# State-space scans of a fused two-layer kernel: three small jobs move between POOL, DVE, ScalarE and TensorE

## The chip, the cores and the metric

One core of a Trainium2 chip runs the whole kernel in one launch. The metric is the device time in microseconds, as the median of several executions. All engines named here are of that core: TensorE (PE, its weight loads PEld), VectorE (DVE), ScalarE (ACT), GpSimd (POOL) and SyncE (SP), which only issues DMAs.

## The reference, cut to what matters

The model has two layers: a tokeniser, attention and a mixture of experts in the first, and in the second a selective state-space block (called attn in the names) and a quantised feed-forward block. There are 16 sequences of 113 tokens with 256 channels, and 16 states per channel. The change touches only the state-space block:

```python
def _L1_attn_ref(x, ...):
    xr = x @ in_proj_w.T + in_proj_b
    x_in, res = jnp.split(xr, 2, axis=-1)
    xc = conv_general_dilated(x_in..., conv_w, ...)      # causal, 4 taps, one filter per channel
    xc = jax.nn.silu(xc + conv_b)
    ssm = xc @ x_proj_w.T + x_proj_b
    delta, Bp, Cp = jnp.split(ssm, [DTRANK, DTRANK + DSTATE], axis=-1)
    delta = jax.nn.softplus(delta @ dt_proj_w.T + dt_proj_b)
    A = -jnp.exp(A_log)
    dA = jnp.exp(delta[..., None] * A)
    dBu = delta[..., None] * Bp[:, :, None, :] * xc[..., None]
    _, ys = jax.lax.associative_scan(op, (dA, dBu), axis=1)   # h[t] = dA[t] * h[t-1] + dBu[t]
    y = (ys * Cp[:, :, None, :]).sum(-1) + xc * D_param
    y = y * jax.nn.silu(res)
    return y @ out_proj_w.T + out_proj_b + (x @ skip_proj_w.T + skip_proj_b)
```

Its input x is the layer-normalised residual, and its result is added to the residual.

## The kernel before

Every engine runs its own program, in program order, and the engines meet only at semaphores. The state-space stage (`pe_ssm`, `act_ssm`, `dve_ssm`, `pool_ssm`) treats the 16 sequences in 8 groups of two; channels lie on partitions as two blocks of 128 (`KT`), and a row of a block holds the 2 x 113 = 226 tokens (`N`) of a group. The 16 states are taken in 8 chunks of two. Groups 1 to 4 run in a hardware loop on PE, ACT and DVE (groups 1 to 6 on POOL), the others are written out.

For chunk c of group g the work goes round the engines like this:

- the spread (PE L1726): two bf16 products with a 0/1 matrix `pick` spread the rows of B for two states over all partitions. B is held in `bc3` as three bf16 parts (high, middle, low) on three blocks of 32 partitions, so that the sum over partitions gives nearly float32.
- the drive (DVE L1242): `dx`, that is delta times xc, times the spread B, 904 wide.
- the decays (ACT L778): two exponentials of delta times A into PSUM. Each waits for the scan of the chunk before, whose place in PSUM it takes.
- the scans (DVE L1252): one per state. They reuse the state buffer of two chunks before and so wait for its read.
- the read (POOL L484): both states times C, 904 wide. It waits for the scans and for the reduction of two chunks before. In chunks 0 to 6 the pair sum (POOL L488, 452 wide) then adds the two halves.
- the reduction (PE L1739): a product with the identity that adds the pair sum to the accumulator in PSUM bank 6. In chunk 7 there is no pair sum and both halves go through TensorE (PE L1744, the double reduction). Each float32 product shows as two MATMUL records.

While group g is scanned, group g+1 (and g+2) is prepared, each piece at a fixed chunk; constants at the top (L49 to L56) set the chunks. In chunk 0 TensorE convolves group g+1 (L1699, 16 records) right after the double reduction that ends group g-1; in chunk 1 come the spread of chunk 2, reduction 0 and the output projection of g-1 (L1760). ScalarE does the two silus in chunk 1 (`silus`, with two table loads, L741 and L749), the projections' evictions in chunk 3 (L755, L757), softplus in chunk 4 (L764 to L769), then the normalised rows of g+2 in chunk 4 (L724), and the eviction of their transposes in chunk 5 (L719). TensorE transposes these rows in chunk 5 (L1679) and projects them in chunks 6 and 7 (L1689). DVE gates the output of g-1 in chunk 1 (L1258), adds it to the residual in chunk 2 (L1263) and after the scans of chunk 5 makes the steps of group g+1: delta (L1233) and dx (L1235), 452 wide. POOL, before its read of chunk 5, splits B of g+1: four instructions on 32 partitions each (L465 to L469), of which the last waits for the second. SP writes C to DRAM and reads it back, spread over the partitions (L418, L422).

In PE's `step` the order inside a chunk is written out:

```python
if c < CHUNKS - 1: spread(g, c + 1, par)
elif more:         spread(g + 1, 0, 1 - par)
if c == 0 and before: reduce(g - 1, CHUNKS - 1, 1 - par)
if more: ... convolve(g + 1) at c == AT_CONV; project_dt(g + 1) at c == AT_DT
if turn_next: ... turn(g + 2) at AT_TURN; project_in(g + 2, par, c - AT_IN) from AT_IN on
if c > 0: reduce(g, c - 1, par)
if before and c == AT_OUT: project_out(g - 1)
```

The opening (group 0) does the same pieces one after the other, and the last group (7) has DVE normalise the rows of the feed-forward block between its scans (L1109).

Of the kernel before, what the change touches and what calls it, by code (L numbers as in the profile page):

```python
# [11 lines left out]
BF16 = mybir.dt.bfloat16  # L12
# [36 lines left out]
AT_CONV, AT_SILU, AT_RANK, AT_RANK_OUT, AT_DT, AT_SOFTPLUS, AT_STEPS = 0, 1, 2, 3, 4, 4, 5  # L49
# [3 lines left out]
AT_NORMALISE, AT_TURN, AT_IN, AT_PAD = 4, 5, 6, 7  # L53
# [46 lines left out]
def build(nc, a, out):  # L100
    ctx = ExitStack()
    with ctx:
# [159 lines left out]
        bc_mid = pl.take((N // 2,), 96).bitcast(BF16)  # L262
# [71 lines left out]
        sp_step, bc_step, bc3_ready, delta_ready, dx_ready = (sem("sp_step"), sem("bc_step"), sem("bc3_ready"), sem("delta_ready"),  # L334
# [124 lines left out]
        def pool_ssm(pool):  # L459
            def split(g, par):  # L460


                pool.wait_ge(proj_ready, 4 * g + 4)
                mid, low = slice(32, 64), slice(64, 96)
                pool.tensor_tensor(bc_rest[low, :], bc[low, :], bc_hi[low, :], ALU.subtract).then_inc(bc_step, 1)  # L465
                pool.tensor_tensor(bc_mid[low, :], bc[low, :], bc_hi[low, :], ALU.subtract).then_inc(bc_step, 1)  # L466
                pool.tensor_tensor(bc3[par][mid, :], bc[mid, :], bc_hi[mid, :], ALU.subtract).then_inc(bc3_ready, 1)
                pool.wait_ge(bc_step, 2 * g + 2)
                pool.tensor_tensor(bc3[par][low, :], bc_rest[low, :], bc_mid[low, :], ALU.subtract).then_inc(bc3_ready, 1)  # L469

            def step(g, par, c_loads, more=True):
                for c in range(CHUNKS):
                    k = g * CHUNKS + c
                    kp = c % 2
                    if more and c == 5:

                        pool.wait_ge(pair_ready, (CHUNKS - 1) * g + c)
                        split(g + 1, 1 - par)
                        pool.wait_ge(bc3_ready, 2 * g + 4)
# [6 lines left out]
                    if c < CHUNKS - 1:  # L486
                        pool.wait_ge(read_ready, k + 3)
                        pool.tensor_tensor(read[kp][:, 0], read[kp][:, 0], read[kp][:, 1], ALU.add).then_inc(pair_ready, 1)  # L488

            pool.wait_ge(pads_zero, 1)  # L490
            split(0, 0)
            pool.wait_ge(bc3_ready, 2)
# [223 lines left out]
        def act_ssm(act):  # L716
# [41 lines left out]

            def softplus(g):
# [21 lines left out]
            def step(g, par, more=True, before=True, turn_next=True):  # L781
                for c in range(CHUNKS):
# [6 lines left out]
                    if more:  # L789
# [4 lines left out]
                        if c == AT_SOFTPLUS:  # L794
                            softplus(g + 1)
                    elif c == 3:
                        act_rstd(act, 5, EARLY_SEQS, load=False)
# [14 lines left out]
            softplus(0)  # L812
            turn(1, 1)
# [393 lines left out]
        def dve_ssm(dve):  # L1207
# [22 lines left out]
            def steps(g, par):  # L1230
                dve.wait_ge(softplus_ready, g + 1)
                dve.wait_ge(xc_ready, KT * g + KT)
                dve.tensor_tensor(delta[par], sp_relu, sp_abs, ALU.add).then_inc(delta_ready, 1)  # L1233
                dve.wait_ge(delta_ready, g + 1)
                dve.tensor_tensor(dx[par], delta[par], xc[par], ALU.mult).then_inc(dx_ready, 1)  # L1235
# [32 lines left out]
            def step(g, par, more=True, before=True, turn_next=True):  # L1268
                for c in range(CHUNKS):
# [6 lines left out]
                    if more and c == AT_STEPS:  # L1276
                        steps(g + 1, 1 - par)
# [20 lines left out]
            steps(0, 0)  # L1298
# [369 lines left out]
        def pe_ssm(pe):  # L1668
# [25 lines left out]
            def convolve(g):  # L1694

                pe.wait_ge(xpad_ready, KT * g + KT)
                for m in range(KT):
# [3 lines left out]
                last.then_inc(conv_ps, 1)  # L1701
# [16 lines left out]
            def spread(g, c, par):  # L1718

                k, kp = g * CHUNKS + c, c % 2  # L1720
                if c == 0:
                    pe.wait_ge(bc3_ready, 2 * g + 2)
# [6 lines left out]
            def reduce(g, c, par):  # L1729
# [7 lines left out]
                if c < CHUNKS - 1:  # L1737
                    pe.wait_ge(pair_ready, (CHUNKS - 1) * g + c + 1)
                    pe.matmul(ps[:, 6, 0:KT * N], ident, read[kp][:, 0].rearrange("p k s -> p (k s)"), start=False,  # L1739
                              stop=False, skip_group_check=True).then_inc(read_used, 1)  # L1740
                else:
                    pe.wait_ge(read_ready, k + 3)
                    for n in range(2):
                        last = pe.matmul(ps[:, 6, 0:KT * N], ident, read[kp][:, n].rearrange("p k s -> p (k s)"), start=False,  # L1744
                                         stop=n == 1, skip_group_check=True)
# [18 lines left out]
            def step(g, par, more=True, before=True, turn_next=True):  # L1764
                for c in range(CHUNKS):
# [8 lines left out]
                    if more:  # L1774
                        if c == (AT_CONV if before else OPENING):
                            convolve(g + 1)
                        if c == AT_DT:
                            project_dt(g + 1)
# [131 lines left out]
```

## Time and profile before

| what | value |
|---|---|
| median of 3 executions | 808.91 us (806.64 to 812.38) |
| the profiled execution, its own time | 809.96 us |
| its span, first to last instruction | 808.2 us |
| mean granted TensorE clock | 0.907 |
| busy: PE / DVE / ACT / POOL | 681.7 / 504.1 / 380.9 / 345.7 us |
| POOL reads, L484 | 124.8 us in 64 |
| DVE scans, L1252 | 133.5 us in 128 |
| the scan stage: DVE from its first drive to its last gate | 455.94 to 732.85 us |

All times of rows are from one profiled execution, counted from the start of its span. The busy time of PE is no measure of how full it is, since its matmuls are pipelined. An idle time stands in brackets with the instruction that ended it. A granted clock of 1 is 2.4 GHz, 0.5 is 1.2 GHz.

### The profile page before, as it was taken

What the parts mean: (1) busy time and instruction counts of PE and PEld (TensorE: products, weight loads), DVE (VectorE), ACT (ScalarE), POOL (GpSimd) and SP (SyncE); (2) the same over time, 40 slices, a digit from 0 to 9 for tenths busy, and PEclk for the clock granted to TensorE, in tenths of its full rate; (3) what the DMA queues carried; (4) which work ended last, traced back from release to release, by engine and by line L of the source; (5) the groups of instructions that cost most, each with busy time, mean ns of one, the idle gap of its engine ahead of it and who ended that gap; (6) DMA issues with size and microseconds to landing.
All of it is one profiled execution on the core that took longest, in us unless ns stands there. A gap on an engine that the chain in (4) does not pass through costs nothing. (4 is left out here: it accounts for less than half of the span.)

```text
span 808.2 us, 11710 instructions
## 1 busy us (share of the span) xinstructions
PE 681.7 (84%) x3673; PEld 456.9 (57%) x3674; DVE 504.1 (62%) x899; ACT 380.9 (47%) x843; POOL 345.7 (43%) x328
## 2 busy tenths in 40 slices
PE   7699999998999979999997688788787895633886
PEld 5478888877666646666655456456455462302444
DVE  1556666665411115444217768988988988995686
ACT  0466667663322122223223575665665764212964
POOL 0012111110276304232230368878878888631336
PEclk9799999997799989999998799999999997756798
DMA  9992000000021251111104220210201202000003
GB/s 266 314 426 112 0 0 0 0 2 1 2 42 23 53 182 47 46 39 46 46 33 99 93 94 1 92 68 26 92 11 82 93 1 93 0 0 0 1 0 92
DMA packets 28836, 52.89 MB, mean 65 GB/s; under 512 B 10975, under 2 KB 23683, under 8 KB 26627
## 3 DMA queue, kind: packets, MB, share of 16 engines
q1 hardware_dynamic: 20067, 47.62, 17.3%
q0 software_dynamic: 8736, 4.85, 2.4%
q8 instruction: 18, 0.29, 0.2%
q14 instruction: 15, 0.12, 0.1%
HBM read 42.75 MB, written 9.60 MB: 65 GB/s over the span
## 5 line engine op out<-in xcount | busy, mean ns | idle before, releaser
L484 POOL TENSOR_TENSOR arena<-arena 128x904 f32<-128x904 f32 x64 | 124.8, 1954 | 59.7 <-DVE arena L1252 53.6
L1252 DVE TENSOR_TENSOR_SCAN arena<-ps,arena 128x452 f32<-128x452 f32 x128 | 133.5, 1084 | 6.7 <-ACT ps L778 2.1
L778 ACT ACTIVATE ps<-arena,sh_w 128x448 f32<-128x448 f32 x128 | 80.3, 635 | 107.3 <-DVE arena L1252 106.4
L1739 PE MATMUL ps<-arena,const 128*128 128x452 f32 x112 | 64.1, 658 | 41.1 <-POOL arena L488 41.1
L1552 PE MATMUL ps<-arena,work 128*128 x176 | 83.3, 598 | 0.0
L558 ACT ACTIVATE work<-ps,work 113x113 f32<-113x113 f32 x256 | 66.8, 387 | 32.6 <-DVE work L909 32.6
L1242 DVE TENSOR_TENSOR arena<-arena,ps 128x904 f32<-128x904 f32 x64 | 69.2, 1081 | 11.0 <-PE ps L1726 10.8
L432 POOL TENSOR_TENSOR xT<-work 128x452 f32<-128x452 f32 x16 | 15.1, 944 | 139.9 <-DVE work L898 139.9
L531 POOL DMA_INDIRECT answers_e<-work,slot_token x22 | 23.7, 1075 | 100.3 <-DVE work L1047 100.3
L488 POOL TENSOR_TENSOR arena<-arena 128x452 f32<-128x452 f32 x56 | 64.1, 1144 | 4.4
L515 POOL DMA_INDIRECT slots_in<-xn,slot x16 | 37.9, 2367 | 58.5 <-issue 58.5
L1508 PE MATMUL ps<-xT,sh_w 128*128 128x452 f32 (+1 forms) x128 | 51.9, 565 | 0.0
L1739 PEld LDWEIGHTS ps<-arena,const 128*128 128x128 f32 x112 | 19.4, 209 | 53.0 <-POOL arena L488 52.9
L1043 DVE TENSOR_TENSOR work<-ps,work 128x512 f32<-128x512 f32 x22 | 15.2, 691 | 52.0 <-PE ps L1552 52.0
L1564 PE MATMUL ps<-arena,work 128*128 x176 | 43.5, 391 | 0.8 <-ACT work L629 0.8
L1552 PEld LDWEIGHTS ps<-arena,work 128*128 128x128 f32 x176 | 31.2, 192 | 22.7 <-issue 22.1
L909 DVE TENSOR_REDUCE work<-ps 113x4 f32<-113x452 f32 x64 | 35.7, 621 | 10.8 <-PE ps L1379 10.8
L1508 PEld LDWEIGHTS ps<-xT,sh_w 128*128 128x128 f32 x128 | 25.3, 199 | 23.9 <-issue 23.5
L1358 PE MATMUL ps<-work 128*128 128x113 f32 x256 | 34.3, 290 | 2.3 <-ACT work L552 1.7
L1564 PEld LDWEIGHTS ps<-arena,work 128*128 128x128 f32 x176 | 32.9, 197 | 5.3 <-issue 1.5
L1689 PE MATMUL ps<-arena,sh_w 128*128 128x226 f32 x128 | 34.7, 425 | 0.9 <-ACT arena L719 0.9
L1385 PE MATMUL ps<-const,work 113*113 113x113 f32 x256 | 33.7, 264 | 1.7 <-ACT work L558 1.7
(245 smaller groups left out, 1364.9 us busy)
## 6 DMA issues: line engine op xcount, KB each, us to landing
arena<-c_rows SPq DMA_DIRECT2D x8, 1808.0 KB, 6.4
arena<-in_ex_w SPq DMA_DIRECT2D x8, 1536.0 KB, 24.4
slots_in<-work SPq DMA_DIRECT2D x1, 2827.0 KB, 23.6
work<-slots_in SPq DMA_DIRECT2D x22, 128.5 KB, 2.1
xn<-answers_e SPq DMA_DIRECT2D x4, 448.0 KB
out<-resid SPq DMA_DIRECT2D x8, 224.0 KB
arena<-in_patches SPq DMA_DIRECT2D x3, 576.0 KB, 6.1
sh_w<-in_sh_w SPq DMA_DIRECT2D x1, 1536.0 KB, 11.7
```

The costliest lines, as they stand in the source:

```text
L484: pool.tensor_tensor(read[kp], state[kp], c_all[par][:, 2 * c:2 * c + 2, :].unsqueeze(2).broadcast_to([P, 2, KT, N]), ALU.mult)\
L488: pool.tensor_tensor(read[kp][:, 0], read[kp][:, 0], read[kp][:, 1], ALU.add).then_inc(pair_ready, 1)
L515: pool.indirect_dma_start(slots_in, bass.IndirectOffsetOnAxis(ap=slot[:, b:b + 1], axis=0), xn2_named[:, b, :], None).then_inc(scattered, 16)
L558: last = act.activation(probs[:, r, j], ps[0:S, 3 + r, j * S:(j + 1) * S], ACT.Exp, bias=negmax[:, h:h + 1])
L778: act.activation(decay_ps(n)[:, :, 1:], delta[par].rearrange("p k (b s) -> p (k b) s", b=GB)[:, :, 1:], ACT.Exp, scale=a_neg[:, 2 * c + n: ...
L909: dve.tensor_reduce(negmax[:, 4 * r:4 * r + 4].unsqueeze(2), ps[0:S, 3 + r, 0:4 * S].rearrange("p (j s) -> p j s", j=4), AX.X, ALU.max, ne ...
L1242: dve.tensor_tensor(drive[kp], dx[par].unsqueeze(1).broadcast_to([P, 2, KT, N]), ps[:, 2 + kp, 0:2 * N].rearrange("p (n s) -> p n s", n=2) ...
L1252: dve.tensor_tensor_scan(state[kp][:, n].rearrange("p k s -> p (k s)"), decay_ps(n).rearrange("p q s -> p (q s)"), drive[kp][:, n].rearran ...
L1508: last = pe.matmul(ps[:, bank, 0:4 * S], sh_w[:, at + k * HID + m * P:at + k * HID + (m + 1) * P], xT2[:, k, bass.ds(g * 4 * S, 4 * S)], s ...
L1552: last = pe.matmul(ps[:, bank, :], xgT[par][:, k, :], arena[:, bass.ds(e * EW + at + k * HID, HID)], start=k == 0, stop=k == KT - 1)
L1564: last = pe.matmul(ps[:, 6, 0:D], e_hT[:, m, :], arena[:, bass.ds(e * EW + DOWN + m * D, D)], start=m == 0, stop=m == HT - 1)
L1739: pe.matmul(ps[:, 6, 0:KT * N], ident, read[kp][:, 0].rearrange("p k s -> p (k s)"), start=False, stop=False, skip_group_check=True).then_ ...
```

## The change

Five edits, all in the state-space stage:

- The split of B. POOL subtracts the high part from all 96 partitions in one instruction (`without_high`, before its read of chunk 4), ScalarE copies the rest to bf16 into the middle and low blocks of `bc3` in two instructions (`middle`, in chunk 5, after the decays of chunk 6 and before the eviction of the transposes), and POOL subtracts the middle part from the low block in place (`without_mid`, before its read of chunk 6). `bc_mid` goes.
- The steps of groups 1 to 7 (delta and dx) run on POOL, before its read of chunk 5, not on DVE. The opening's stay on DVE.
- Pair sums are kept only in chunks 0 to 4 (`PAIRED`). In chunks 5, 6 and 7 TensorE adds both halves.
- ScalarE normalises the rows of g+2 in chunk 3, not 4 (`AT_NORMALISE`), which is now before softplus.
- The convolution of g+1 is done one channel block in chunk 0 and the other in chunk 1, so that the spread of chunk 2 stands between them (in group 0 it is still whole, in chunk 1).

```diff
-AT_CONV, AT_SILU, AT_RANK, AT_RANK_OUT, AT_DT, AT_SOFTPLUS, AT_STEPS = 0, 1, 2, 3, 4, 4, 5
+AT_REST, AT_MID, AT_LOW = 4, 5, 6
+PAIRED = 5
+AT_SILU, AT_RANK, AT_RANK_OUT, AT_DT, AT_SOFTPLUS, AT_STEPS = 1, 2, 3, 4, 4, 5
...
-AT_NORMALISE, AT_TURN, AT_IN, AT_PAD = 4, 5, 6, 7
+AT_NORMALISE, AT_TURN, AT_IN, AT_PAD = 3, 5, 6, 7
...
         def pool_ssm(pool):
-            def split(g, par):
+            low = slice(64, 96)
+
+            def without_high(g):
                 pool.wait_ge(proj_ready, 4 * g + 4)
-                mid, low = slice(32, 64), slice(64, 96)
-                pool.tensor_tensor(bc_rest[low, :], bc[low, :], bc_hi[low, :], ALU.subtract).then_inc(bc_step, 1)
-                pool.tensor_tensor(bc_mid[low, :], bc[low, :], bc_hi[low, :], ALU.subtract).then_inc(bc_step, 1)
-                pool.tensor_tensor(bc3[par][mid, :], bc[mid, :], bc_hi[mid, :], ALU.subtract).then_inc(bc3_ready, 1)
-                pool.wait_ge(bc_step, 2 * g + 2)
-                pool.tensor_tensor(bc3[par][low, :], bc_rest[low, :], bc_mid[low, :], ALU.subtract).then_inc(bc3_ready, 1)
+                pool.tensor_tensor(bc_rest, bc, bc_hi, ALU.subtract).then_inc(bc_rest_ready, 1)
+
+            def without_mid(g, par):
+                pool.wait_ge(bc_mid_ready, g + 1)
+                pool.tensor_tensor(bc3[par][low, :], bc_rest[low, :], bc3[par][low, :], ALU.subtract).then_inc(bc3_ready, 1)
+
+            def steps(g, par):
+                pool.wait_ge(softplus_ready, g + 1)
+                pool.wait_ge(xc_ready, KT * g + KT)
+                pool.tensor_tensor(delta[par], sp_relu, sp_abs, ALU.add).then_inc(delta_ready, 1)
+                pool.wait_ge(delta_ready, g + 1)
+                pool.tensor_tensor(dx[par], delta[par], xc[par], ALU.mult).then_inc(dx_ready, 1)
 
             def step(g, par, c_loads, more=True):
                 for c in range(CHUNKS):
                     k = g * CHUNKS + c
                     kp = c % 2
-                    if more and c == 5:
-
-                        pool.wait_ge(pair_ready, (CHUNKS - 1) * g + c)
-                        split(g + 1, 1 - par)
-                        pool.wait_ge(bc3_ready, 2 * g + 4)
+                    if more and c == AT_REST:
+                        without_high(g + 1)
+                    if more and c == AT_STEPS:
+                        steps(g + 1, 1 - par)
+                    if more and c == AT_LOW:
+                        pool.wait_ge(read_ready, k + 2)
+                        without_mid(g + 1, 1 - par)
+                        pool.wait_ge(bc3_ready, g + 2)
...
-                    if c < CHUNKS - 1:
+                    if c < PAIRED:
                         pool.wait_ge(read_ready, k + 3)
                         pool.tensor_tensor(read[kp][:, 0], read[kp][:, 0], read[kp][:, 1], ALU.add).then_inc(pair_ready, 1)
...
+            def middle(g, par):
+                act.wait_ge(bc_rest_ready, g + 1)
+                act.activation(bc3[par][32:64, :], bc_rest[32:64, :], ACT.Copy)
+                act.activation(bc3[par][64:96, :], bc_rest[64:96, :], ACT.Copy).then_inc(bc_mid_ready, 1)
...
+                        if c == AT_MID:
+                            middle(g + 1, 1 - par)
...
             softplus(0)
+            middle(0, 0)
             turn(1, 1)
...
-                    if more and c == AT_STEPS:
-                        steps(g + 1, 1 - par)
...
-                pe.wait_ge(bc3_ready, 2 * g + 2)
+                pe.wait_ge(bc3_ready, g + 1)
...
-                if c < CHUNKS - 1:
-                    pe.wait_ge(pair_ready, (CHUNKS - 1) * g + c + 1)
+                if c < PAIRED:
+                    pe.wait_ge(pair_ready, PAIRED * g + c + 1)
...
-                        if c == (AT_CONV if before else OPENING):
+                        if not before and c == OPENING:
                             convolve(g + 1)
+                        if before and c < KT:
+                            convolve(g + 1, (c,))
```

## Rows read from the trace of the kernel before

**Rows 1.** Page, costliest groups: count, busy us, mean ns, idle before, releaser.
```profile
L484 POOL TENSOR_TENSOR arena<-arena 128x904 f32<-128x904 f32 x64 | 124.8, 1954 | 59.7 <-DVE arena L1252 53.6
```

**Rows 2.** Chain that ended last, in order of time: start us, us, what.
```profile
475.53 1.95 POOL arena L484
...
493.49 1.80 PE ps L1744 x4
...
506.85 1.96 POOL arena L484
...
588.63 1.80 PE ps L1744 x4
...
601.97 1.95 POOL arena L484
...
620.31 1.80 PE ps L1744 x4
...
633.33 1.94 POOL arena L484
```

**Rows 3.** Timeline of POOL in group 4: start us, us, what, idle before.
```profile
607.22 1.14 POOL L488 TENSOR_TENSOR arena<-arena 128x452 f32<-128x452 f32 x1
608.54 1.06 POOL L465 TENSOR_TENSOR arena<-arena 32x226 f32<-32x226 f32 x1 [0.18 <-POOL arena L488]
...
610.60 0.57 POOL L467 TENSOR_TENSOR arena<-arena 32x226 bf16<-32x226 f32 x1
...
612.05 1.95 POOL L484 TENSOR_TENSOR arena<-arena 128x904 f32<-128x904 f32 x1 [0.23 <-POOL arena L469]
...
615.17 1.95 POOL L484 TENSOR_TENSOR arena<-arena 128x904 f32<-128x904 f32 x1
```

**Rows 4.** Timeline of DVE, same stretch.
```profile
593.70 1.10 DVE L1242 TENSOR_TENSOR arena<-arena,ps 128x904 f32<-128x904 f32 x1 [0.53 <-PE ps L1726]
...
597.08 0.69 DVE L1263 TENSOR_TENSOR resid<-ps,resid 113x512 f32 x1
...
599.81 2.09 DVE L1252 TENSOR_TENSOR_SCAN arena<-ps,arena 128x452 f32<-128x452 f32 x2
...
603.02 2.09 DVE L1252 TENSOR_TENSOR_SCAN arena<-ps,arena 128x452 f32<-128x452 f32 x2
...
608.52 0.63 DVE L1233 TENSOR_TENSOR arena<-arena 128x452 f32<-128x452 f32 x1 [0.21 <-ACT arena L769]
609.18 0.90 DVE L1235 TENSOR_TENSOR arena<-arena 128x452 f32<-128x452 f32 x1
```

**Rows 5.** Timeline of ScalarE in group 4.
```profile
602.84 1.09 ACT L757 ACTIVATE arena<-ps,sh_w 96x226 f32<-96x226 f32 x3
...
607.81 0.58 ACT L769 ACTIVATE arena<-arena 128x452 f32<-128x452 f32 x1
608.30 1.08 ACT L724 ACTIVATE arena<-resid,shift,rstd 113x256 f32 x2
```

**Rows 6.** Timeline of TensorE in group 4 and start of the next group.
```profile
609.51 0.60 PE L1679 MATMUL ps<-const,arena 113*128 113x113 f32 x4 [2.23 <-ACT arena L724]
...
616.33 1.71 PE L1689 MATMUL ps<-arena,sh_w 128*128 128x226 f32 x8
...
621.94 3.22 PE L1699 MATMUL ps<-arena,xT 128*128 128x226 f32 x16
```

**Rows 7.** Windows of TensorE: stretch, us, busy (count), granted clock, DMA, GB/s.
```profile
610.00:613.80 3.80, 3.80 (x13) 0.55 0.06 27
...
677.50:684.90 7.40, 6.49 (x11) 0.50 0.01 2
```

**Rows 8.** Timeline of DVE in the last group.
```profile
714.25 0.85 DVE L1109 TENSOR_SCALAR xn<-resid,mean,rstd 113x256 f32<-113x256 f32 x1
...
715.47 0.40 DVE L1109 TENSOR_SCALAR xn<-resid,mean,rstd 113x256 f32<-113x256 f32 x1
```

**Rows 9.** Timeline of DVE at the opening.
```profile
455.94 1.10 DVE L1242 TENSOR_TENSOR arena<-arena,ps 128x904 f32<-128x904 f32 x1
```

More of the change, by code:

```diff
@@ L261, in build @@
         bc_hi = pl.take((N // 2,), 96).bitcast(BF16)
-        bc_mid = pl.take((N // 2,), 96).bitcast(BF16)
         bc3 = [pl.take((N // 2,), 96).bitcast(BF16) for _ in range(2)]
@@ L333, in build @@
         proj_ps, proj_ready, dt_ps, softplus_ready = sem("proj_ps"), sem("proj_ready"), sem("dt_ps"), sem("softplus_ready")
-        sp_step, bc_step, bc3_ready, delta_ready, dx_ready = (sem("sp_step"), sem("bc_step"), sem("bc3_ready"), sem("delta_ready"),
+        sp_step, bc_rest_ready, bc_mid_ready, bc3_ready, delta_ready, dx_ready = (sem("sp_step"), sem("bc_rest_ready"), sem("bc_mid_ready"), sem("bc3_ready"), sem("delta_ready"),
                                                               sem("dx_ready"))
@@ L490, in pool_ssm @@
             pool.wait_ge(pads_zero, 1)
-            split(0, 0)
-            pool.wait_ge(bc3_ready, 2)
+            without_high(0)
+            without_mid(0, 0)
+            pool.wait_ge(bc3_ready, 1)
             step(0, 0, 16)
@@ L1228, in normalise, with opening_steps @@
                                       ALU.subtract, ALU.mult).then_inc(xn3_ready, 1)
[L1230 to L1235, printed above, removed]
+            def opening_steps():
+                dve.wait_ge(softplus_ready, 1)
+                dve.wait_ge(xc_ready, KT)
+                dve.tensor_tensor(delta[0], sp_relu, sp_abs, ALU.add).then_inc(delta_ready, 1)
+                dve.wait_ge(delta_ready, 1)
+                dve.tensor_tensor(dx[0], delta[0], xc[0], ALU.mult).then_inc(dx_ready, 1)
             def drives(g, c, par):
@@ L1297, in dve_ssm @@
             dve.wait_ge(decay_zero, 2)
-            steps(0, 0)
+            opening_steps()
             step(0, 0, before=False)
@@ L1692, in project_in, with convolve @@
                         last.then_inc((xin_ps, res_ps)[m // KT], 1)
-            def convolve(g):
+            def convolve(g, blocks=range(KT)):
                 pe.wait_ge(xpad_ready, KT * g + KT)
-                for m in range(KT):
+                for m in blocks:
                     for t in range(TAPS):
@@ L1700, in convolve @@
                                          start=t == 0, stop=t == TAPS - 1, skip_group_check=True)
-                last.then_inc(conv_ps, 1)
+                if KT - 1 in blocks:
+                    last.then_inc(conv_ps, 1)
             def project_x(g, par):
@@ L1744, in reduce @@
                         last = pe.matmul(ps[:, 6, 0:KT * N], ident, read[kp][:, n].rearrange("p k s -> p (k s)"), start=False,
-                                         stop=n == 1, skip_group_check=True)
+                                         stop=c == CHUNKS - 1 and n == 1, skip_group_check=True)
                     last.then_inc(read_used, 1)
```

## The prediction, made before the changed kernel was run

> **What bounds the kernel now.** I read the page's costliest groups first: the longest of POOL's, 64 products of 1.95 us at L484, sits idle 59.7 us, and 53.6 us of that end with a scan of DVE [rows 1]. So POOL is near the bound of the scan stage, but it and DVE wait for each other in turn. Which wait ends last where is in the chain in order of time. It repeats once per group: POOL's read of chunk 3 starts at 506.85 and, four groups on, at 633.33, so a period is 126.48 / 4 = 31.62 us [rows 2]. I measure inside a group from the start of that read (R = 0; for group 4 this is 601.97).
>
> Half of the period is POOL's. From R = 0 TensorE's last reduction (chunk 7) starts at 620.31 - 601.97 = 18.34 [rows 2]. A read with its pair sum takes 3.12 us (612.05 to 615.17), a read alone 1.95, and the four instructions of the split push the next read to 612.05 - 607.22 = 4.8 us after the start of a pair sum, where 1.1 is usual (the sum's own 1.14, slightly overlapped): 3.7 us [rows 3]. 4 x 3.12 + 3.7 + 1.95 = 18.1: POOL has no pause in this half.
>
> The other half is a relay: from the start of reduction 7 to the next read 3 it is 633.33 - 620.31 = 13.02 (13.36 from group 0 to 1) [rows 2]. In it TensorE does the reduction, the convolution, a spread, reduction 0 and the output projection; the residual add at 597.08 starts 8.45 us after reduction 7 of the group before (588.63), then it is 2.7 until scan 3 at 599.81 and 2.16 until the read at 601.97 [rows 2, 4]. DVE's cadence is 3.2 per chunk (599.81 to 603.02) [rows 4]; eight of them, 1.5 of steps and some 2 of gate and residual add are about 29: DVE has some 2 us of air.
>
> **The change, part by part, per group.**
> Split. POOL loses four instructions (3.7 us) and gets one of 96 x 226 and one of 32 x 226. The trace has no 96-partition one. The 32 x 226 ones took 0.57 alone and 1.06 beside DVE's steps [rows 3]; the pair sum of 128 x 452 took 1.14 [rows 3] and bounds it from above. The steps leave DVE, so I take 0.65 and 0.6, with 0.1 + 0.2 of own-semaphore waits: 1.5 in all, ends 1.3 and 2.4. ScalarE gets two copies; three like ones took 1.09 [rows 5], so 0.75. They stand behind softplus and the decays of chunk 6 (two of 0.64, near R = 7.9 at the end), so they end near R = 8.6; POOL asks for them at 11.3, with reads 6 and 7 queued behind that wait: 2.7 of cover, cost 0. The same copies put off ScalarE's eviction of the transposes to 9.1 and the first half projection on TensorE to 9.2 to 10.9; reduction 5 behind it is wanted at 11.3, so 0.4 of cover, bound 0.3.
> Steps. DVE loses 0.63 + 0.90 [rows 4]. POOL gets two 128 x 452 instructions: at the pair sum's 1.14 with the 0.08 wait between, 2.4; ends 1.3 (DVE's price) and 4 (twice the 1.95 of a 904-wide read, all the contention I can imagine). They wait for softplus, which ended at 608.39 = R + 6.4 [rows 5]; normalising a chunk ahead now goes before it, 1.08 us [rows 5]; ScalarE waited there for the scans of chunk 4 before, which I reckon hides all but 0.3, so R + 6.7. POOL gets there at 6.9. Nearly a tie, with read 5 behind the wait: cost 0, bound 0.5.
> Pair sums. Chunks 5 and 6 lose theirs (7 keeps its two products): 2 x 1.17 (3.12 - 1.95) off POOL. TensorE gets one more product pair for each; a double reduction holds it 621.94 - 620.31 = 1.63 [rows 2, 6], some 0.8 more than a single one.
> POOL then: pairs 3 and 4, 6.24; high part 0.7; steps 2.4; read 5, 1.95: read 5 ends at R = 11.3 instead of about 15.1 in old order. Low part with waits 0.9, reads 6 and 7: 16.0 instead of 18.25. DVE's scan 7 needs read 5 (it reuses its buffer), starts at 11.4, ends 13.5, in time for read 7 at 14.0.
> What is late next is TensorE. From the end of read 5 it does reduction 5 (1.63), spread (0.2), half a projection (1.6; span 1.71 [rows 6]), reduction 6 (1.63), spread (0.2), then reduction 7: 5.3 us without a gap, so 16.6, not 16.0. The start of reduction 7 moves from 18.34 to 16.6: **1.75 us gained per group**.
> Convolution in halves. Drive 2 waited 0.53 for its spread behind the 3.22 of the convolution [rows 4, 6]. The half moved behind the spread lets scan 2 begin 0.6 earlier. But the residual add then waits for the output projection, whose TensorE work before it is unchanged: it starts 8.4 after reduction 7 as before. So 0, with a gain of up to 0.6 as the other end. The silus begin after both halves, within 0.1 of when ScalarE is free; cost 0, bound 0.35.
> Rows a chunk ahead. TensorE's transposes waited 2.2 us for them with a reduction behind them [rows 6]. Nobody on the path waited, so 0 directly; but the granted clock fell to the low level right after that idle time (0.55 over 610.0 to 613.8) [rows 7]. By the order of its queue its idle pieces become some 1.2 us before reduction 4, 1.2 behind it and 0.4 before reduction 5, and I take the 5.3 us above at the high level.
> The SP queue is not touched: its loads of C start from the projections, and the read 0 that wants them comes at R = 16.7.
>
> Outside the five periods: group 0's first part was 493.49 - 475.53 = 17.96 [rows 2], gain 1.45. Group 6 has no turn and no projection, TensorE idles 3.2 us before reduction 5, and ran all of its late reductions at 0.50 [rows 7]: double reductions then cost up to 3.3, and I take 1.4 instead of 1.75. Group 7 is DVE's: in chunks 5 and 6 one normalising instruction each lasted 0.85, ending with POOL's pair sum, against 0.40 for the next one [rows 8]; without the sums 2 x 0.45 = 0.9. The opening pays: the split's last instruction now waits for two copies behind softplus; spread 0 is ready near 456.4 and the drive that began at 455.94 [rows 9] starts about 0.6 later.
> **Sum:** 5 x 1.75 + 1.45 + 1.4 + 0.9 - 0.6 = 11.9 us. The profiled execution took 809.96 (span 808.2 and 1.8 around it), so 798.1; its time is 1.05 over the median of 808.91, which would give 797.0. I say 797.5.
>
> Two rules weighed against these rows. An elementwise 128 x 452 costs POOL 1.14 and DVE 0.63 [rows 3, 4], and where the two met, DVE's product rose from 0.63 to 0.90 and POOL's small ones from about 0.6 to 1.0 [rows 3, 4]. The Trainium skill (GPSIMD Engine Reference, 4.1 Engine selection) advises against this very move: two-input elementwise work belongs on VectorE, POOL being about twice as slow. The trace agrees, with 1.8 times. By that rule alone the moved steps would lose: POOL pays 2.4 in the half that it bounds, and DVE saves 1.5 where it had air; the sum is a gain only by the 2.3 of the pair sums and the 2.2 of the split. The Trainium skill (SBUF — State Buffer, SBUF: two separate sides) says that a DVE instruction with two SBUF inputs and a POOL instruction shut each other out. The slowed rows fit; by it the moved steps run at 1.14, since scans and drives take an input from PSUM, and the upper end of 4 falls away.
>
> **Rivals.**
> A. The thin covers break: POOL waits 0.5 for softplus, the 96-row instruction costs 0.5 more, and reduction 5 comes 0.3 late. All of it lies ahead of the end of read 5, so nothing absorbs it: of 1.75 some 0.5 is left. 7 x 0.5 + 0.3 = 3.8: about 806. For it: covers of 0.2 and 0.4 us. Against: ScalarE's and POOL's durations vary by hundredths.
> B. DVE and POOL gain more: if reduction 6 keeps off reduction 7's way and the relay shortens by the 0.6 of the convolution, 2.9 per group, 7 x 2.9 + 0.3: 789. For it: scan 2 is earlier. Against: the output projection stands behind the same products.
> C. Slower. TensorE's clock falls in its idle time before reduction 5 and stays low as in group 6, 7.4 us at 0.50 [rows 7], over reductions 5 to 7 and half the convolution. That adds 3.7 per group to the path, 3.7 - 1.75 = 1.95 lost, six times = 12, less 0.3: about 821. It decides once the low stretch within the path is over 3.5 us; one like 610 to 613.8 (3.8 us, costing 1.9) just cancels the gain, 809. For it: the clock did fall once per group. Against: it fell after 2.2 us of idleness, and the new pieces are shorter with work between.
> D. The change does not do what it says (POOL still full to the end of read 7): 808, unlikely, as the pair sums go in any case.
>
> **Chances.** The forecast 0.60, A 0.15, B 0.08, C with its half case 0.12, D 0.05. Its range is 790 to 807: B's end with the lower bounds of the small terms, A's on the other. About 1%, 8 us, is what a measurement of this kernel tells from none. Over 1% faster means under 800.8: forecast but for a part (0.53), B (0.08), a part of A (0.05): 0.66. Within 1%: the rest of A and of the forecast, D, the half of C: 0.26. Slower by over 1%: 0.08.
>
> **What would show it.** Right: period of read 3 near 29.8; reduction 7 starting 16.6 after read 3; steps on POOL 1.14 each; TensorE unbroken from read 5 to reduction 7; residual add still 8.4 after reduction 7 with DVE idle before it. Wrong: POOL idle before the delta sum, or TensorE's half projection still running when read 5 ends (A); granted clock below 1 between reductions 5 and 7 in the looped groups (C); residual add with no wait (B); a pair of DVE scans longer than 2.09 or a POOL read longer than 1.95 would be contention that I did not count.

## The result: 10 us faster, and where they came from

The changed kernel takes 800.60 us (median of 4 runs, 799.70 to 802.37) against 810.64 (4 runs, 806.64 to 812.64) for the kernel before on the same chip: 0.9885 of its time, 95% interval 0.9844 to 0.9925. The profiled execution took 799.85 us with a span of 798.0, against 809.96 and 808.2.

First the page of the kernel after: its chain by engine and the line of the reads, which answers to [rows 1].

```profile
span 798.0 us, 11738 instructions
...
PE 17%; DVE 9%; ACT 8%; issue 5%; POOL 3%; DVEq 0%; ACTq 0%; POOLq 0%
...
L494 POOL TENSOR_TENSOR arena<-arena 128x904 f32<-128x904 f32 x64 | 124.8, 1950 | 66.6 <-DVE arena L1271 59.2
```

POOL's reads are as long as before, but POOL has 3% of the chain that ended last, where it had 15%, and PE has 17% instead of 5%. The path has changed engines. How much work changed engines is in the stretch from read 3 of group 0 to read 3 of group 7, seven periods. Before and after (columns: busy time and instructions of PE, PEld, DVE, ACT, POOL; then the granted clock):

```profile
475.53:695.91 220.38, 177.27 (x683) 112.08 (x682) 198.25 (x212) 134.28 (x249) 185.82 (x133) 0.93 0.15 60
```

```profile
473.67:686.34 212.67, 183.62 (x711) 120.42 (x711) 187.13 (x198) 138.28 (x263) 171.65 (x119) 0.94 0.16 62
```

POOL does 14.2 us less and DVE 11.1 less, yet the stretch is only 7.7 shorter, 1.1 per period instead of the 1.66 forecast on average (11.6 / 7). TensorE is busy 6.4 more, and a third of the gain is missing. Group 4 of the kernel after shows it. R = 0 is its read 3, at 596.16. First the timeline of POOL (columns as in [rows 3]):

```profile
599.29 0.58 POOL L465 TENSOR_TENSOR arena<-arena 96x226 f32<-96x226 f32 x1
...
602.95 1.15 POOL L474 TENSOR_TENSOR arena<-arena 128x452 f32<-128x452 f32 x1
604.18 1.14 POOL L476 TENSOR_TENSOR arena<-arena 128x452 f32<-128x452 f32 x1
605.26 1.95 POOL L494 TENSOR_TENSOR arena<-arena 128x904 f32<-128x904 f32 x1
607.29 0.61 POOL L469 TENSOR_TENSOR arena<-arena 32x226 bf16<-32x226 f32 x1
608.12 1.94 POOL L494 TENSOR_TENSOR arena<-arena 128x904 f32<-128x904 f32 x1 [0.23 <-POOL arena L469]
610.43 1.94 POOL L494 TENSOR_TENSOR arena<-arena 128x904 f32<-128x904 f32 x1 [0.38 <-PE ps L1762]
```

The high part took 0.58 (forecast 0.65), the steps 1.15 and 1.14 (1.14), the low part 0.61 (0.6). None of them waited for softplus or the copies. Read 5 ends at 607.21 = R + 11.05; the forecast was 11.3. POOL's side is as reckoned. But the last row waits for TensorE. Its timeline from there, which answers to [rows 6]:

```profile
603.05 1.03 PE L1757 MATMUL ps<-arena,const 128*128 128x452 f32 x2 [1.20 <-POOL arena L498]
...
605.29 3.31 PE L1706 MATMUL ps<-arena,sh_w 128*128 128x226 f32 x8 [1.02 <-ACT arena L730]
608.39 1.89 PE L1762 MATMUL ps<-arena,const 128*128 128x452 f32 x4
...
610.32 1.71 PE L1706 MATMUL ps<-arena,sh_w 128*128 128x226 f32 x8
611.87 1.68 PE L1762 MATMUL ps<-arena,const 128*128 128x452 f32 x4
...
613.58 1.70 PE L1762 MATMUL ps<-arena,const 128*128 128x452 f32 x4
```

And the windows of the same core over that place, which answer to [rows 7] (PEclk is the column behind POOL):

```profile
600.00:605.00 5.00, 3.08 (x16) 1.70 (x14) 4.74 (x6) 4.88 (x12) 4.84 (x4) 1.00 0.85 344
605.00:606.00 1.00, 0.71 (x2) 0.67 (x3) 1.00 (x2) 0.97 (x3) 1.00 (x2) 0.70 0.00 0
606.00:607.00 1.00, 1.00 (x4) 0.88 (x4) 0.70 (x1) 0.46 (x1) 1.00 (x1) 0.50 0.00 0
607.00:608.00 1.00, 1.00 (x4) 0.90 (x3) 0.59 (x1) 0.00 (x0) 0.82 (x2) 0.50 0.00 0
```

The two halves of the projection are the same eight records. The second lasts 1.71, the first 3.31: it runs at the low level (0.50 of full speed, 1.2 GHz), after two idle pieces of 1.20 and 1.02 us. So it still runs at 607.21, when read 5 is done, and reduction 5 begins at R + 12.23 instead of some 11.1. The low level is not new there. In the kernel before the same half of group 4 lasted 2.50 us:

```profile
611.81 2.50 PE L1689 MATMUL ps<-arena,sh_w 128*128 128x226 f32 x8
```

TensorE then still idled 0.97 before its next reduction, so this cost nothing. In the kernel after that spare time is gone. From the slow half on TensorE has no gap, and reduction 7 starts at 613.58 = R + 17.42, where 16.6 was forecast and 18.34 was before.

The relay behind reduction 7 is unchanged. DVE's rows, the gate and the residual add, which answer to [rows 4]:

```profile
615.31 0.63 DVE L1277 TENSOR_TENSOR arena<-ps,arena 128x452 f32<-128x452 f32 x1 [0.44 <-PE ps L1762]
...
621.83 0.69 DVE L1282 TENSOR_TENSOR resid<-ps,resid 113x512 f32<-113x512 f32 x1 [0.78 <-PE ps L1778]
```

The residual add starts 8.25 us after reduction 7 and waits 0.78 for TensorE; the next read 3 comes at 626.50, 12.92 after reduction 7 (before 13.02). The chain in order of time (start, us, what) says the same in one piece, with ScalarE's second copy and its eviction ahead of the slow half:

```profile
604.28 0.39 ACT arena L773
604.69 0.56 ACT arena L730
605.29 3.31 PE ps L1706 x8
608.60 1.69 PE ps L1762 x4
```

The bound of this half of the period was POOL's queue; now it is ScalarE's eviction, then TensorE's queue.

The account of the 10.2 us between the two spans, one execution of each kernel (the four times of the kernel before lie 6 us apart, so its small terms are not all due to the change): seven periods -7.7; the last group from read 3 to its gate 36.94 to 36.06, -0.88; from POOL's first split instruction to read 3 of group 0, 24.59 to 23.33, -1.26; the work before the state-space stage -0.6; the last output projection and its residual add +1.78; what follows them -1.5. The +1.78 is the clock again (0.50 from 723 to 727 us), in the timeline of PE at the end of the kernel after:

```profile
718.98 3.38 PE L1762 MATMUL ps<-arena,const 128*128 128x452 f32 x4 [4.12 <-POOL arena L494]
723.09 3.76 PE L1778 MATMUL ps<-sh_w,arena 128*113 128x256 f32 x8 [0.72 <-DVE arena L1277]
```

The same eight products took 1.89 in the loop, and 1.98 at the end of the kernel before.

### The profile page after: what moved, and what is told of

It reads as the page before. It is cut to its first block and busy times, and to the rows that moved or that the text cites. A ratio compares the mean times of both kernels' runs of the same rounds, so it can differ in the third digit from the quotient of the medians.

```text
span 798.0 us, 11738 instructions
## 1 busy us (share of the span) xinstructions
PE 685.9 (86%) x3705; PEld 462.7 (58%) x3706; DVE 491.1 (62%) x885; ACT 385.6 (48%) x859; POOL 328.9 (41%) x310
## 5 line engine op out<-in xcount | busy, mean ns | idle before, releaser
L1271 DVE TENSOR_TENSOR_SCAN arena<-ps,arena 128x452 f32<-128x452 f32 x128 | 133.7, 1087 | 11.6 <-POOL arena L494 4.4
L433 POOL TENSOR_TENSOR xT<-work 128x452 f32<-128x452 f32 x16 | 15.1, 942 | 139.1 <-DVE work L917 139.1
L1762 PE MATMUL ps<-arena,const 128*128 128x452 f32 x96 | 49.4, 643 | 14.8 <-POOL arena L494 14.8
L1757 PE MATMUL ps<-arena,const 128*128 128x452 f32 x80 | 40.7, 591 | 24.8 <-POOL arena L498 24.7
L498 POOL TENSOR_TENSOR arena<-arena 128x452 f32<-128x452 f32 x40 | 45.7, 1143 | 3.1
L1569 PEld LDWEIGHTS ps<-arena,work 128*128 128x128 f32 x176 | 31.2, 192 | 22.7 <-issue 22.1
L1706 PE MATMUL ps<-arena,sh_w 128*128 128x226 f32 x128 | 38.2, 458 | 6.5 <-ACT arena L730 6.5
L1762 PEld LDWEIGHTS ps<-arena,const 128*128 128x128 f32 x96 | 21.4, 235 | 30.4 <-POOL arena L494 18.1
L1706 PEld LDWEIGHTS ps<-arena,sh_w 128*128 128x128 f32 x128 | 30.3, 248 | 10.2 <-ACT arena L730 8.4
```

The source lines that it names most:

```text
L1271: dve.tensor_tensor_scan(state[kp][:, n].rearrange("p k s -> p (k s)"), decay_ps(n).rearrange("p q s -> p (q s)"), drive[kp][:, n].rearran ...
L1569: last = pe.matmul(ps[:, bank, :], xgT[par][:, k, :], arena[:, bass.ds(e * EW + at + k * HID, HID)], start=k == 0, stop=k == KT - 1)
L1706: last = pe.matmul(ps[:, 1 - m // KT, m % KT * N:(m % KT + 1) * N], in_w[:, k, m * P:(m + 1) * P], x3T[par][:, k, :], start=k == 0, stop=k ...
```

## Experiments

Ratios are to the kernel before on the same chip; the kernel after stood at 0.9885.

### Is the slow half of the projection what is missing?

**e6_evict_first**: ScalarE evicts the transposes before the decays of chunk 6 and before the two copies.

```diff
 # act_ssm, chunk loop of the kernel after
+                    if turn_next and c == AT_TURN:
+                        turn(g + 2, par)
...
-                        if c == AT_TURN:
-                            turn(g + 2, par)
```

> Only change: ScalarE evicts the transposed rows before the decays of chunk 6 and the copies of the split, not after them. Theory: TensorE's half projection starts at 8.1 after read 3 instead of 9.1; whether or not its clock falls, it ends near 11.1, so reduction 5 follows read 5 at once; reduction 7 at 16.4, period 29.3, about 794. Rival: the decays of chunk 6, now 0.55 later, hold scan 6 and the chain goes over ScalarE; no gain, 800 or more.

Measured 792.50 (791.11 to 793.16), ratio 0.9784, interval 0.9747 to 0.9821. The periods are 29.45, 29.43, 29.44, 29.43, 29.12, 29.11 and 28.95. Group 4 in the timeline of PE (read 3 at 591.62):

```profile
599.80 1.71 PE L1706 MATMUL ps<-arena,sh_w 128*128 128x226 f32 x8
602.74 1.79 PE L1762 MATMUL ps<-arena,const 128*128 128x452 f32 x4 [1.23 <-POOL arena L494]
...
607.82 1.70 PE L1762 MATMUL ps<-arena,const 128*128 128x452 f32 x4
```

The first half starts at R + 8.18, is done before read 5 ends (TensorE idles 1.23 us for that read), and reduction 7 starts at R + 16.20. That chain is 5.08 long, where the forecast had 5.3. The window of 8 us around it:

```profile
600.00:604.00 4.00, 2.77 (x12) 1.83 (x12) 3.85 (x4) 2.60 (x5) 3.70 (x4) 1.00 0.00 0
604.00:608.00 4.00, 4.00 (x19) 2.85 (x18) 3.97 (x5) 2.59 (x5) 3.45 (x2) 1.00 0.00 0
```

In group 4 the clock did fall, but earlier (0.51 from 595.5 to 598.75) and off the path: its period is 29.12 against 29.11 in group 5, where it did not fall. This version beats both kernels. But the half here is both earlier and fast; the next run parts the two.

**e7_fill**: small bf16 products, 60 columns wide, are added to TensorE's two idle pieces (10 in chunk 5, 8 ahead of the first half projection). They write unused columns of the accumulator's bank. The output of the block is another with them, so this run serves for times only; the rest of the work is as after.

```diff
+FILLS = (10, 8)
...
+            def fill(products):
+                for _ in range(products):
+                    pe.matmul(ps[:, 6, KT * N:512], pick[:, 0, :], pick[:, 0, 0:512 - KT * N], start=True, stop=True,
+                              skip_group_check=True)
```

> Base is the changed kernel (read 3 to read 3: 30.34 us in the last looped group; reduction 7 starts 17.42 after read 3; the first half projection lasts 3.31 at the low clock). 18 short products that compute nothing are put in TensorE's two pauses of chunks 5 and 6, ahead of that projection. Theory 'clock': the granted clock no longer falls there, the half projection lasts about 1.7, reduction 5 starts when read 5 ends (11.1 after read 3 instead of 12.2), reduction 7 at 16.4, period 29.3, the whole about 6 us less: 794. Rival 'queue': the projection is late because of where it stands and not because of its clock; the fill changes nothing or costs its own length (0.5 us per group), 800 to 804.

Measured 799.95 (797.00 to 804.09), ratio 0.9884, interval 0.9831 to 0.9937: no faster than after, so as a cure it failed. In groups 0 to 4 the clock fell all the same (the half lasted 3.05 to 3.22); in groups 3 and 4 reduction 7 came at R + 17.41 and 17.42, and the periods were 30.67 and 30.34. In group 5 it did not fall, and that group is the cleanest evidence of all (read 3 at 627.27; windows, then timeline of PE):

```profile
637.00:642.00 5.00, 4.83 (x22) 3.52 (x21) 4.18 (x5) 2.55 (x6) 4.70 (x4) 1.00 0.00 0
```

```profile
636.40 1.80 PE L1712 MATMUL ps<-arena,sh_w 128*128 128x226 f32 x8 [0.81 <-ACT arena L731]
638.37 1.79 PE L1768 MATMUL ps<-arena,const 128*128 128x452 f32 x4 [0.17 <-POOL arena L495]
...
643.45 1.70 PE L1768 MATMUL ps<-arena,const 128*128 128x452 f32 x4
```

The half starts at R + 9.13, exactly where it does after, but lasts 1.80, and reduction 7 comes at 16.18 and the period is 29.10. With the same order and the same start, the clock alone makes 1.24 us of a group (17.42 - 16.18). In group 5 of e6 the half starts 1.2 us earlier and the period is 29.11, no shorter than these 29.10: the earlier start by itself adds nothing.

**e8_project_early**: as e6, and the two halves of the projection stand a chunk earlier, in chunks 5 and 6.

```diff
-AT_NORMALISE, AT_TURN, AT_IN, AT_PAD = 3, 5, 6, 7
+AT_NORMALISE, AT_TURN, AT_IN, AT_PAD = 3, 5, 5, 7
...
-                        if c >= AT_IN:
+                        if c in (AT_IN, AT_IN + 1):
```

> Eviction first as in e6_evict_first, and both half projections a chunk earlier (chunks 5 and 6 instead of 6 and 7). Theory: no projection stands between reductions 5 and 7 any more; POOL's reads 6 and 7 become the bound again; reduction 7 starts at 15.9 to 16.1 after read 3, period 28.9, about 791. Rival: reduction 4 and the spread of chunk 7 now stand behind a projection, drive 7 is late by up to 0.5 and the clock falls elsewhere; 794 to 797.

Measured 793.12 (791.13 to 795.60), ratio 0.9795, interval 0.9751 to 0.9838: the same as e6. In groups 1 to 5 reduction 7 came at R + 15.82 to 15.88 and the six first periods were 0.2 to 0.4 shorter, but read 3 of group 0 came 1.4 later (475.26 against 473.87) and the seventh period took 30.62 instead of 28.95. What the loop gained, its two ends gave back.

**e9_tail_fill**: e6 with products in bank 0 (96 x 384) ahead of reduction 5 of group 6 (15) and in the last group (10 behind reduction 5 and 18 behind reduction 6), to hold up the clock where the late groups idle.

```diff
+                    if more and not turn_next and c == 6:
+                        pe.wait_ge(proj_ready, 4 * GROUPS)
+                        fill(FILLS[0])
...
+                    if not more and c >= 6:
+                        fill(FILLS[c - 5])
```

> e6_evict_first with products that compute nothing put on TensorE where it idled at the end of the stage: 15 in group 6 before reduction 5, 10 and 18 in group 7 behind reductions 5 and 6, all into bank 0, which is free there. Theory: the last double reduction (3.38 at the low clock) and the last output projection (3.76) run at the high clock, 1.7 and 1.9, and group 6 saves 0.3: 792.5 - 3.7 = 789. Rival: the fill itself is still running when read 7 ends and gives back what the clock gains: 791 to 794.

Measured 792.72 (792.26 to 794.14), ratio 0.9804, interval 0.9778 to 0.9830: no gain over e6. In group 6 it did what it was to do (reduction 5 in 1.78 instead of 3.20, period 27.97 instead of 28.95), but the end got worse. PE in e9, then in e6:

```profile
705.30 3.09 PE L1724 MATMUL ps<-xT 96*128 96x384 bf16 x18
711.06 2.64 PE L1767 MATMUL ps<-arena,const 128*128 128x452 f32 x4 [2.67 <-POOL arena L495]
714.42 3.75 PE L1783 MATMUL ps<-sh_w,arena 128*113 128x256 f32 x8 [0.72 <-DVE arena L1278]
```

```profile
711.44 3.38 PE L1762 MATMUL ps<-arena,const 128*128 128x452 f32 x4 [4.01 <-POOL arena L494]
715.55 1.98 PE L1778 MATMUL ps<-sh_w,arena 128*113 128x256 f32 x8 [0.72 <-DVE arena L1277]
```

With the fill the clock fell later, within the last double reduction, and lay at 0.50 over the projection. The rows of after above have nearly e6's history (4.12 idle, 3.38, 0.72 idle) and still 3.76 where e6 has 1.98. What tips it is open.

### Which part of the change pays?

Four parts of the kernel after were undone one at a time, and two were made alone in the kernel before.

**e5_conv_whole**: the convolution in one piece again.

```diff
-                        if before and c < KT:
-                            convolve(g + 1, (c,))
+                        if before and c == 0:
+                            convolve(g + 1)
```

> The changed kernel with the convolution whole again, in chunk 0 before the spread of chunk 2. Theory: drive 2 waits about 0.5 for its spread again, but the residual add waits for the output projection anyway, so its start (8.3 after reduction 7) and the period (30.3 to 30.6) stay: 800.6 within 1. Rival: the split of the convolution carried up to 0.6 per group, and undoing it costs 4 us: 804.5.

Measured 800.89 (797.58 to 803.38), ratio 0.9877, interval 0.9829 to 0.9926. The periods are those of after to 0.05 us, but for the first, which is 0.11 longer. Read 2 came at R + 25.7 instead of 25.15, and the next read 3 no later. The halves are worth nothing that these runs show.

**e1_pairs_back**: chunks 5 and 6 have their pair sums on POOL again.

```diff
-PAIRED = 5
+PAIRED = 7
...
-                        pool.wait_ge(read_ready, k + 2)
+                        pool.wait_ge(pair_ready, PAIRED * g + c)
```

> The changed kernel with pair sums in chunks 0 to 6 again. Theory: POOL's two extra sums (1.17 each) put the end of read 7 from 15.9 to 18.1 after read 3, past what TensorE's late queue hides, so reduction 7 starts at 18.2 instead of 17.4: period 31.1, and group 7 loses its 0.9: about 806. Rival: TensorE's queue is the bound, and with single reductions it is relieved by 1.6; no loss, 800.

Measured 813.84 (10 runs, 811.25 to 816.49), ratio 1.0061, interval 1.0033 to 1.0089: 1.8% above the kernel after, far more than expected. The seven periods sum to 224.8 against 212.7. Four of them are 31.0 to 31.7 long, the other three 33.0 to 33.2. The short ones are about as long as expected (31.1): reduction 7 comes at R + 18.2 to 18.4. In the long ones the half projection was fast (1.80) and the clock fell later, over reduction 7 itself:

```profile
589.92 1.03 PE L1757 MATMUL ps<-arena,const 128*128 128x452 f32 x2 [1.27 <-POOL arena L498]
...
591.82 3.37 PE L1762 MATMUL ps<-arena,const 128*128 128x452 f32 x4 [0.68 <-POOL arena L494]
```

**e2_steps_dve**: the steps go back to DVE, after the scans of chunk 5.

```diff
 # pool_ssm
-                    if more and c == AT_STEPS:
-                        steps(g + 1, 1 - par)
 # dve_ssm, behind the scans
+                    if more and c == AT_STEPS:
+                        steps(g + 1, 1 - par)
```

> The changed kernel with the steps of all groups on DVE again. Theory: reads 5 to 7 end earlier on POOL or at the same time, but TensorE comes free for reduction 5 only at 12.2 after read 3 (half projection at the low clock), so reduction 7 stays at 17.4 and the period at 30.3 to 30.7: 800.6 within 2; the move of the steps was worth nothing by itself. Rival 1: POOL still sets the path, and 2.4 less on it gives 1 per group: 794. Rival 2: DVE becomes the bound, 1 more per group: 807.

Measured 806.63 (10 runs, 804.65 to 808.93), ratio 0.9963, interval 0.9945 to 0.9980. Not the 1.5 us of [rows 4] came back to DVE, but twice that. DVE, then POOL:

```profile
606.50 0.63 DVE L1250 TENSOR_TENSOR arena<-arena 128x452 f32<-128x452 f32 x1 [0.39 <-ACT arena L783]
607.16 2.25 DVE L1252 TENSOR_TENSOR arena<-arena 128x452 f32<-128x452 f32 x1
```

```profile
606.57 2.36 POOL L492 TENSOR_TENSOR arena<-arena 128x904 f32<-128x904 f32 x1
```

The product of 0.63 lasts 2.25, and ends 0.48 after POOL's read, which itself lasts 2.36 instead of 1.95. The other way round, the moved steps beside DVE's scans and drives took 1.15 and 1.14: as long as a pair sum alone. Behind the product DVE's queue is the bound: POOL's read 6 waits for its scans, and read 7 another 1.26.

```profile
612.72 1.95 POOL L492 TENSOR_TENSOR arena<-arena 128x904 f32<-128x904 f32 x1 [2.83 <-DVE arena L1269]
```

Reduction 7 comes at R + 18.16 against 17.42. An estimate: 1.62 earlier, with the product at its 0.63, it would come at 16.5, ahead of the kernel after, so the lengthened product is enough to account for the loss.

**e3_split_back**: the split in four instructions on 32 partitions, behind the steps on POOL; ScalarE's copies go.

```diff
+                pool.tensor_tensor(bc_rest[low, :], bc[low, :], bc_hi[low, :], ALU.subtract).then_inc(bc_rest_ready, 1)
+                pool.tensor_tensor(bc_mid[low, :], bc[low, :], bc_hi[low, :], ALU.subtract).then_inc(bc_rest_ready, 1)
+                pool.tensor_tensor(bc3[par][mid, :], bc[mid, :], bc_hi[mid, :], ALU.subtract).then_inc(bc3_ready, 1)
+                pool.wait_ge(bc_rest_ready, 2 * g + 2)
+                pool.tensor_tensor(bc3[par][low, :], bc_rest[low, :], bc_mid[low, :], ALU.subtract).then_inc(bc3_ready, 1)
```

> The changed kernel with the four-instruction split on POOL again, before its read of chunk 5, behind the steps. Theory: read 5 ends at 13.7 after read 3 instead of 11.1, reduction 5 starts then instead of at 12.2, reduction 7 at 18.8 instead of 17.4: period 31.7, about 809. Beside no step on DVE the four instructions last 0.57 to 0.6 each, not 1.0. Rival: ScalarE is relieved of two copies and evicts the rows 0.8 earlier, so the clock does not fall and half of the loss is won back: 804.

Measured 823.75 (822.99 to 825.69), ratio 1.0173, interval 1.0143 to 1.0203. It lost more than twice what was expected. POOL's six instructions in a row (the two steps and the split) hold read 5 back (its end is at R + 13.73, as expected), TensorE idles 3.77 us, and the low clock behind that lies over the critical chain (group 4, read 3 at 609.26):

```profile
623.04 2.26 PE L1758 MATMUL ps<-arena,const 128*128 128x452 f32 x4 [3.77 <-POOL arena L494]
...
625.47 2.78 PE L1702 MATMUL ps<-arena,sh_w 128*128 128x226 f32 x8
```

**e4_rows_back**: the rows are normalised in chunk 4 again.

```diff
-AT_NORMALISE, AT_TURN, AT_IN, AT_PAD = 3, 5, 6, 7
+AT_NORMALISE, AT_TURN, AT_IN, AT_PAD = 4, 5, 6, 7
```

> The changed kernel with the rows normalised in chunk 4, behind softplus, again. Theory: the eviction and with it the half projection of chunk 6 come about 1 us later; reduction 7 follows by 1: period 31.3 to 31.4, about 806. Rival: nobody on the path waits for the rows and the clock falls in either case: 800.6 within 1.

Measured 802.75 (6 runs, 798.92 to 806.20), ratio 0.9914, interval 0.9882 to 0.9945. That overlaps with the kernel after. Four periods are 29.8 to 30.6 and the last is 29.0, but two are above 32 (reduction 5 at the low level, reduction 7 at R + 19.4 and 19.2). The medians lie 0.3% apart; whether moving the rows ahead is worth anything, these runs don't settle.

**b1_pairs_only**: the kernel before, without the pair sums of chunks 5 and 6.

```diff
+PAIRED = 5
...
-                    if c < CHUNKS - 1:
+                    if c < PAIRED:
```

> The kernel before with one edit alone: pair sums only in chunks 0 to 4. Theory: read 5 ends at 12.0 after read 3, TensorE needs 5.1 from there to reduction 7, so 17.1 instead of 18.3: period 30.4, with 0.9 in group 7 about 9 us less than before: 800. Rival: the double reductions 5 and 6 fall into the low clock that follows the idle time before the transposes, 1.5 more: no gain, 809.

Measured 802.52 (801.43 to 803.85), ratio 0.9917, interval 0.9887 to 0.9948. This one edit gives 0.83% of the whole change's 1.15%, in periods of 29.9 to 30.6; the intervals overlap, so what the other four edits add together is not clear of noise. Reduction 7 came at R + 17.15 in group 4, as expected (17.1). In groups 0 to 3 the clock fell and the half projection lasted 2.8 to 3.4; in groups 4 and 5 it did not fall. In group 4 (read 3 at 598.13) the idle piece of 2.23 is still there, and the clock stays at 1.00:

```profile
605.66 0.60 PE L1680 MATMUL ps<-const,arena 113*128 113x113 f32 x4 [2.23 <-ACT arena L725]
...
607.13 1.80 PE L1690 MATMUL ps<-arena,sh_w 128*128 128x226 f32 x8
610.20 1.79 PE L1745 MATMUL ps<-arena,const 128*128 128x452 f32 x4 [1.28 <-POOL arena L485]
```

**b2_steps_only**: the kernel before, with the steps on POOL behind the split.

```diff
 # pool_ssm, behind split(g + 1, 1 - par)
+                        steps(g + 1, 1 - par)
 # dve_ssm
-                    if more and c == AT_STEPS:
-                        steps(g + 1, 1 - par)
```

> The kernel before with one edit alone: the steps on POOL, behind the split. Theory: POOL bounds this half, pays 2.4 and wins back 0.8 because its split no longer meets DVE's steps: reduction 7 at 19.9 after read 3 instead of 18.3, period 33.2, six or seven times 1.6: about 820. Rival: as in the changed kernel without this edit, DVE's product was what cost, and POOL's extra is hidden: 809 or less.

Measured 825.85 (822.16 to 826.72), ratio 1.0195, interval 1.0158 to 1.0232; the expectation had 820. The two steps take 2.1 us, but the split without DVE's steps beside it takes 0.9 less, so read 5 ends only 1.26 later than before (R + 13.29 against 12.03). The rest is the clock (group 4, read 3 at 612.48):

```profile
627.04 1.88 PE L1745 MATMUL ps<-arena,const 128*128 128x452 f32 x2 [3.76 <-POOL arena L496]
...
629.09 3.25 PE L1695 MATMUL ps<-arena,sh_w 128*128 128x226 f32 x8
```

Read 7 ends at R + 19.53, 1.24 later than before, but TensorE is still busy with what these slow records put off, and reduction 7 comes at R + 20.86, 2.5 later than before: half of it is POOL's longer queue and half the clock. Set against e2, the move of the steps costs some 16 us alone (1.95%) and is worth 6 (0.9963 against 0.9885) in the company of the other edits. That the pair sums and the split are what made the room is argued from the queues; no run has the steps with one of them alone. The parts don't add up; each changes what the others meet.

## Why the prediction was right, and where its sizes were off

The forecast was 797.5 us, the result 800.6, within the range. Point by point:

- **POOL's half, and what is late next.** Shown. Read 5 ended at R + 11.05 (11.3), the moved instructions cost what was put down, and TensorE's queue from read 5 to reduction 7 took over as the bound. With the clock up it is 5.08 long (e6, e7's group 5), and reduction 7 comes at R + 16.2, 0.4 before the forecast. The 15.1 given for the end of read 5 in the old order is a slip: the read at 612.05 [rows 3] is read 5, and it ended at 614.00 = R + 12.03; 15.1 is read 6. The sum does not use it.
- **The step that was mis-sized** is "the first half projection on TensorE to 9.2 to 10.9". It began at R + 9.13, but took 3.1 us of TensorE instead of 1.6, so the cover of 0.4 became a delay of 1.1. The five looped periods together gained 4.9 us, 1.0 each, instead of 5 x 1.75 = 8.75. Its length was taken from the second half's row [rows 6]; the first half's own row in that timeline had 2.50. The reason given against rival C, shorter idle pieces with work between, did not hold: the clock fell behind pieces of 1.20 and 1.02 us. It is rival C in small, at a price of 1.2 per group instead of 3.7, since the low stretch lay over the half projection and ended within reduction 5. Rival A's sign (the half projection still running when read 5 ends) was seen too, and of its causes the late reduction 5, at 1.1 us for 0.3. The other two were not: POOL did not wait for softplus, and the 96-row instruction took 0.58.
- **Group 6.** Gain 1.97 (31.45 to 29.48), forecast 1.4; TensorE ran at 0.50 there as before. **Group 0** gained 0.79 (31.32 to 30.53) for 1.45: the same term as in the loop.
- **Group 7.** Gain 0.88 for 0.9: the normalising instruction [rows 8] took 0.41 instead of 0.85, in chunks 5 and 6.
- **Opening.** Forecast +0.6; the drive came 0.15 later relative to POOL's first split instruction. What followed, up to read 3, was 1.41 shorter; the clock there was 1.00 against 0.86 (460 to 472 us in both), but no run tests whether that is why. Not foreseen, and neither were the +1.78 of the last output projection and the 2.1 less before the stage and behind it.
- **How much of the agreement is luck.** The periods and the last group were to give 12.5 us and gave 8.6. The other 1.6 of the 10.2 between the spans, where the forecast had -0.6, come from the opening and from places that it did not speak of. Without them the profiled execution would have missed the sum by 3.9 us and not by 1.7 (the medians miss the forecast by 3.1).
- **Convolution in halves at 0.** Borne out by e5. The residual add starts 8.25 after reduction 7 and waits for TensorE: shown.
- **Rows ahead at 0, with the worry about the clock.** Open (e4).

On the rule weighed in the prediction. The Trainium skill (GPSIMD Engine Reference, 4.1 Engine selection) would leave the steps on VectorE. b2 bears it out: the move alone loses 16 us, about half of it by POOL's longer queue. In the changed kernel it fails, because undoing the move (e2) loses 6. There DVE's instruction does not cost its 0.63: it lasts 2.25 beside a read on POOL. The Trainium skill (SBUF — State Buffer, SBUF: two separate sides) has the two shut each other out, and these rows agree: in all seven places beside a read the product ends 0.48 to 0.50 after that read does, so most of its 0.63 comes behind it; in the opening of e2, with no read beside it, it took 0.63. The prediction used that rule only for the price on POOL (upper end 4 dropped; measured 2.3), and did not turn it round to ask what DVE was spared.

## What to carry to other kernels

When an engine's queue is shortened, write out the next engine's queue from the same event, with the granted clock of each piece of it: the same eight records cost 1.7 or 3.3 us here, and that was the main error. A stretch at the low level that is covered in the kernel before can lie on the path after. If a thin cover hangs on an eviction, put the eviction ahead of copies that have slack; one call moved brought 8 us more. And price a move between DVE and POOL in the order in which the other edits leave the two queues: the same move was worth -16 and +6 us here.

## What the runs showed of the hardware that was not expected

- A DVE product of two SBUF operands, 0.63 us by itself, took 2.25 or 2.26 in the seven places in e2 where it met a POOL read, which also grew, from 1.95 to 2.33 and more. Moved to POOL, beside scans and drives, neither side lengthened.
- On POOL 96 x 226 took 0.58 and 32 x 226 took 0.57: the number of partitions made no difference.
- The granted clock. In the looped groups of the kernel after it fell after two idle pieces of 1.2 and 1.0 us with 1.2 us of products between them; in b1 it fell behind a piece of 2.23 in groups 1 to 3 and stayed up through one of 2.23 and one of 1.28 in group 4; in e7, with the same products added in each group, it fell in groups 0 to 4 and not in 5; and at the end of e6 and of after, nearly the same history led to 1.98 and 3.76 for the same eight products. So the rows of one execution don't give a rule for when it falls here; what its fall costs they do give, close to a factor of two on the products under it (3.38 against 1.79 for a double reduction).
